# Weights and tables of five stages loaded during the stage in front of each

## The reference

```
for each layer:
    xn = layernorm(x)
    s  = attention(xn)
    g  = silu(ffn(xn))
    x  = x + s * g
```

## Time and profile before

| what | us |
|---|---|
| median of 3 runs (lowest, highest) | 6142.15 (6142.1, 6144.57) |
| the profiled execution | 6135.76 |
| its span, first to last instruction | 6134.0 |
| busy in the span: PE, DVE, ACT, POOL | 5688.0, 4321.5, 3850.9, 2914.1 |
| f0: first row load issued to last scatter begun | 1117.45 to 1221.32 |
| a1: first part load issued | 1228.42 |
| f1: first row load issued | 1976.35 |
| a2: first row load issued | 3558.97 |
| f2: first row load issued | 5439.89 |
| a3: first row load issued | 5653.05 |
| f3: first transpose | 5963.6 |

### The profile page before, as it was taken

One profiled execution on the slowest core, in us unless ns is written; L12 is line 12 of the kernel. 1 busy time (PEld: TensorE's weight loads), 2 busy tenths in 40 slices (PEclk: granted clock), 3 DMA queues, 4 the chain that ended last, 5 costly groups with the idle time before them and its releaser, 6 DMA issues. The chain is left out here.

```text
span 6134.0 us, 102245 instructions
## 1 busy us (share of the span) xinstructions
PE 5688.0 (93%) x33833; PEld 3013.5 (49%) x33833; DVE 4321.5 (70%) x9755; ACT 3850.9 (63%) x8213; POOL 2914.1 (48%) x2774
## 2 busy tenths in 40 slices
PE   8999999689997999999999979999999999987868
PEld 3444444422222566666666634444444444455558
DVE  4555555178885777777888768888888888867655
ACT  2444444256665677777777757777777777755436
POOL 1224326456776766666666533323323323324458
PEclk9999999799998999999999989999999999999879
DMA  2001001221110111111111110000000000013123
GB/s 47 15 15 39 26 15 45 75 58 40 32 35 30 42 30 34 32 32 39 40 46 46 34 35 11 13 19 11 13 19 11 13 19 11 11 43 116 45 95 97
DMA packets 304270, 219.34 MB, mean 36 GB/s; under 512 B 27890, under 2 KB 279668, under 8 KB 303492
## 3 DMA queue, kind: packets, MB, share of 16 engines
q1 hardware_dynamic: 284578, 177.38, 11.2%
q0 software_dynamic: 12544, 29.71, 1.4%
q10 hardware_dynamic: 6626, 5.72, 0.3%
HBM read 97.11 MB, written 73.87 MB: 28 GB/s over the span
## 5 line engine op out<-in xcount | busy, mean ns | idle before, releaser
L3864 PE MATMUL a_scores_ps<-a_kT,a_q_mixed 128*128 128x512 f32 x2048 | 1046.4, 593 | 3.2 <-ACT a_probs L3674 3.1
L3874 PE MATMUL a_acc_ps<-a_probsT,a_v_post 128*128 128x512 f32 x2048 | 1042.8, 592 | 0.4 <-DVE a_probsT L3767 0.4
L3674 ACT ACTIVATE a_probs<-a_scores_ps,a_neg_max 128x512 f32<-128x512 f32 x1024 | 703.0, 687 | 428.6 <-DVE a_neg_max L3757 419.3
L3757 DVE TENSOR_REDUCE a_neg_max<-a_scores_ps 128x1 f32<-128x512 f32 x1024 | 693.4, 677 | 202.0 <-PE a_scores_ps L3864 196.9
L3767 DVE STREAM_TRANSPOSE a_probsT<-a_probs 128x512 f32<-128x512 f32 x1024 | 715.5, 699 | 135.9 <-PE a_acc_ps L3874 112.5
L3679 ACT ACTIVATE a_probs<-a_probs,a_inv_sum 128x512 f32<-128x512 f32 x1024 | 727.7, 711 | 0.8 <-DVE a_inv_sum L3762 0.8
L3045 DVE TENSOR_REDUCE a_neg_max<-a_pair_ps 128x2 f32<-128x1024 f32 (+3 forms) x512 | 417.7, 824 | 354.5 <-PE a_pair_ps L3141 349.4
L2850 ACT ACTIVATE a_probsT<-a_pair_ps 128x1024 f32<-128x1024 f32 (+3 forms) x512 | 359.4, 704 | 484.4 <-PE a_pair_ps L3154 482.9
L3874 PEld LDWEIGHTS a_acc_ps<-a_probsT,a_v_post 128*128 128x128 f32 x2048 | 389.0, 190 | 490.9 <-issue 488.8
L3864 PEld LDWEIGHTS a_scores_ps<-a_kT,a_q_mixed 128*128 128x128 f32 x2048 | 384.4, 190 | 476.0 <-issue 438.2
L3620 POOL TENSOR_TENSOR a_q_mixed<-a_qT,a_pre 128x512 f32<-128x512 f32 x248 | 250.1, 1040 | 759.7 <-PE a_scores_ps L3864 759.7
(11 more groups left out here) (420 smaller groups left out, 11863.5 us busy)
## 6 DMA issues: line engine op xcount, KB each, us to landing
f_v_even<-f_v_odd SPq DMA_DIRECT2D x224, 130.0 KB, 2.3
a_v<-a_v_rows SPq DMA_DIRECT2D x256, 64.0 KB, 2.1
f_x_tiles<-routed_x SPq DMA_DIRECT2D x72, 193.0 KB
attention_out<-a_s_out SPq DMA_DIRECT2D x48, 256.0 KB, 2.3
routes_y_rows<-a_zeros SPq DMA_DIRECT2D x32, 256.0 KB, 2.8
a_parts<-routes_y_rows SPq DMA_DIRECT2D x32, 256.0 KB, 3.4
f_x<-x_after SPq DMA_DIRECT2D x32, 256.0 KB
f_gx<-x_after SPq DMA_DIRECT2D x32, 256.0 KB, 3.1
```

What stands on the lines that cost most here:

```text
L3674: act.activation(probs[:, n % NPR, :], scores_ps[n % NS][:], ACT.Exp, bias=neg_max[:, n % NS:n % NS + 1], scale=1.0, accum_out=row_sum[:, ...
L3757: dve.tensor_reduce(neg_max[:, n % NS:n % NS + 1], scores_ps[n % NS][:], AX.X, ALU.max, negate=True).then_inc(max_ready, 1)
L3864: pe.matmul(scores_ps[n % NS][:], q_mixed[:, g % 2, i].rearrange("f a q -> f (a q)"), kT[:, par, :], start=True, stop=True).then_inc(score ...
L3874: pe.matmul(acc_ps[par][:], v_post[:, g, i, :], probsT[:, g % NT, i, :], start=(p == 0), stop=(p == U - 1)).then_inc(products_done, 1)
```

## The change

A class `Ahead` holds tiles, a semaphore and a list of loads. For f0, a1, f1, a2 and a3 a function makes it before the stage in front begins, and that stage issues the loads on SP, one for each body of its loop, and waits for them at its end. The stages take their tiles from it and no longer load or wait for them, ACT issues none. w_o, w1 and w2 of f1's first layer stay in f1 (three loads behind the rows, waited for by TensorE in the second item's body), a3 keeps the load of the identity, and f2 keeps its six loads. In a3 DVE does the scaling of the query weights and the gate's norm first (without a wait), then the first rows' moments, then the rest of its set-up. The numbers of loads issued ahead are 4 in a0, 8 in f0, 11 in a1, 13 in f1 and 10 in f2.

The diff, cut to its core:

```diff
+class Ahead:
+    def __init__(self, nc, ctx, tag, shapes):
+        self.tiles = {name: ctx.enter_context(nc.sbuf_tensor(f"{tag}_{name}", shape, F32))
+                      for name, shape in shapes.items()}
+        self.loaded = nc.alloc_semaphore(f"{tag}_loaded")
+        self.loads = []
+    def take(self, names):
+        return [self.tiles[name] for name in names.split()]
+    def load(self, eng, n):
+        if 0 <= n < len(self.loads):
+            dst, src = self.loads[n]
+            eng.dma_start(dst, src).then_inc(self.loaded, 16)
+    def all_loaded(self, eng):
+        eng.wait_ge(self.loaded, 16 * len(self.loads))
+
+def dispatched_experts_weights(nc, ctx, dram):
+    ahead = Ahead(nc, ctx, "f0", {"ident": [P, P], "w1": [D, 16, P], "w2": [P, 16, D], "expert": [P, NB * NC]})
+    ident, w1, w2, expert = ahead.take("ident w1 w2 expert")
+    ahead.loads = [(ident[:], dram["ident"]), (expert[:], dram["L0f_expert"]), (w1[:], dram["L0_w1"]),
+                   (w2[:], dram["L0_w2"])]
+    return ahead
...
 a1, SP:
             load_parts(0)
-            sp.dma_start(*loads[0]).then_inc(weights, 16)
-            sp.wait_ge(parts_loaded[0], 64)
-            for dst, src in loads[2::2]:
-                sp.dma_start(dst, src).then_inc(weights, 16)
-
             load_parts(1)
             store_x(0)
             def body(j, n):
                 if n <= LAST - 3:
                     load_parts(n + 3)
+                following.load(sp, n - 1)
                 if n >= 1:
...
             bodies(sp, body)
             sp.wait_ge(x_stored, 16 * batches)
+            following.all_loaded(sp)
 a1, ACT:
-            act.wait_ge(parts_loaded[0], 64)
-            for dst, src in loads[1::2]:
-                act.dma_start(dst, src).then_inc(weights, 16)
 a1, TensorE:
-            pe.wait_ge(weights, 16 * len(loads))
 f1, SP:
             rows.load(sp, 0, 0)
-            sp.dma_start(*loads[0]).then_inc(weights, 16)
-            sp.wait_ge(rows.x_loaded, 16)
-            for dst, src in loads[2::2]:
-                sp.dma_start(dst, src).then_inc(weights, 16)
+            sp.dma_start(w_o[:, 0], dram["L1_wo"][0]).then_inc(ffn_weights, 16)
+            sp.dma_start(w1[:, 0], dram["L1_w1"][0]).then_inc(ffn_weights, 16)
+            sp.dma_start(w2[:, 0], dram["L1_w2"][:, 0]).then_inc(ffn_weights, 16)
...
                 for c in range(STEPS):
+                    if c == 1:
+                        following.load(sp, n - 4)
 f1, TensorE:
-            pe.wait_ge(weights, 16 * len(loads))
+                    if n == 1 and c == 0:
+                        pe.wait_ge(ffn_weights, 48)
 a3, SP:
             load_x(0)
-            sp.dma_start(*loads[0]).then_inc(weights, 16)
-            sp.wait_ge(x_loaded[0], 16)
-            for dst, src in loads[2::2]:
-                sp.dma_start(dst, src).then_inc(weights, 16)
+            sp.dma_start(ident[:], dram["ident"]).then_inc(ident_loaded, 16)
             for b in range(1, min(4, batches)):
                 load_x(b)
 a3, DVE:
-            dve.memset(v[:], 1.0).then_inc(pads, 1)
-            dve.wait_ge(weights, 16 * len(loads))
             dve.tensor_scalar(w_in[:, 0, :], w_in[:, 0, :], SCORE_SCALE, None, ALU.mult).then_inc(w_scaled, 1)
             chain(dve.tensor_tensor(wg_sq[:], wg[:], wg[:], ALU.mult))
             dve.tensor_reduce(wg_norm[:], wg_sq[:], AX.X, ALU.add).then_inc(gate_weights, 1)
-            dve.memset(carry[:], 0.0)
...
             moments_of(0)
+            dve.wait_ge(gate_weights, 3)
+            chain(dve.tensor_scalar(wg_norm[:], wg_norm[:], 1e-4, None, ALU.max))
+            chain(dve.reciprocal(wg_norm[:], wg_norm[:]))
+            dve.tensor_scalar(wg_unit[:], wg[:], wg_norm[:], None, ALU.mult).then_inc(gate_weights, 1)
+            dve.memset(v[:], 1.0).then_inc(pads, 1)
+            dve.memset(carry[:], 0.0)
+            dve.memset(no_counts[:], 0.0)
+            dve.tensor_copy(rows[:, :, :, HOME], home[:].rearrange("p (b c) -> p b c", c=NC)).then_inc(tails_ready, 1)
+            chain(dve.memset(fill[:], 0.0))
+            dve.memset(fill[:, HOME:HOME + 1], float(routed_rows.NOWHERE)).then_inc(fill_ready, 1)
 f2, SP:
             def body(j, n):
+                following.load(sp, n - 1)
 a0, SP:
             def body(j, n):
+                following.load(sp, n - 2)
 f0, SP:
             for g in range(4, GROUPS):
                 sp.dma_start(x[:, g], routes.x_groups[g]).then_inc(loaded[g], 16)
+            for n in range(len(following.loads)):
+                following.load(sp, n)
+            following.all_loaded(sp)
             sp.wait_ge(rows_scattered, 16 * GROUPS * NC)
 f0, ACT:
-            act.dma_start(ident[:], dram["ident"]).then_inc(weights, 16)
-            act.dma_start(expert[:], dram["L0f_expert"]).then_inc(weights, 16)
-            act.dma_start(w1[:, 0:PER * K], dram["L0_w1"][:, 0:PER * K]).then_inc(weights, 16)
-            act.dma_start(w2[:, 0:PER * K], dram["L0_w2"][:, 0:PER * K]).then_inc(weights, 16)
-            act.dma_start(w1[:, PER * K:], dram["L0_w1"][:, PER * K:]).then_inc(weights, 16)
-            act.dma_start(w2[:, PER * K:], dram["L0_w2"][:, PER * K:]).then_inc(weights, 16)
...
 program:
+    with ExitStack() as f1_ctx:
+        f1_weights = streamed_transformer_weights(nc, f1_ctx, dram)
+        with ExitStack() as a1_ctx:
+            a1_weights = paired_attention_weights(nc, a1_ctx, dram)
+            with ExitStack() as f0_ctx:
+                f0_weights = dispatched_experts_weights(nc, f0_ctx, dram)
+                causal_attention_phase(nc, dram, "a0", x_in, s, routes, batches, f0_weights)
+                dispatched_experts_phase(nc, "f0", routes, f0_weights, a1_weights)
+            paired_attention_phase(nc, "a1", x_in, x1, s, routes, batches, a1_weights, f1_weights)
+        a2_weights = mixed_attention_weights(nc, f1_ctx, dram)
+        streamed_transformer_phase(nc, dram, "f1", x1, s, x2, batches, f1_weights, a2_weights)
+        mixed_attention_phase(nc, "a2", x2, s, batches, a2_weights)
...
```

More of the change, by code:

```diff
@@ new lines, in dispatched_experts_weights, with paired_attention_weights @@
+def dispatched_experts_weights(nc, ctx, dram):
[4 more added lines that the diff above has]
+    return ahead
+def paired_attention_weights(nc, ctx, dram):
+    S, W = 8, 64
+    ahead = Ahead(nc, ctx, "a1", {"ident": [P, P], "wq": [D, S, 2, W], "wk": [D, 2, 2, 2, W], "wv": [D, D]})
+    ident, wq, wk, wv = ahead.take("ident wq wk wv")
+    ahead.loads = [(ident[:], dram["ident"]), (wv[:], dram["L1_Mv"])]
+    ahead.loads += [(wq[:, :, twice, :], dram["L1_Mq"].rearrange("d (s w) -> d s w", s=S)) for twice in range(2)]
+    k_columns = dram["L1_Mk"].rearrange("d (rho half a w) -> d rho half a w", rho=2, half=2, a=2)
+    ahead.loads += [(wk[:, :, a, half, :], k_columns[:, :, half, a, :]) for a in range(2) for half in range(2)]
+    return ahead
@@ new lines, in upper_attention_weights @@
+def upper_attention_weights(nc, ctx, dram, batches):
+    E, GR = 8, 16
+    TILES = dram["L3f_tile_no"].shape[1]
+    ahead = Ahead(nc, ctx, "a3", {
+        "w_in": [D, 3, D], "below": [P, T], "w_gate": [D, GR], "wg": [E, GR], "rank": [P, E], "place": [P, E],
+        "home": [P, batches * NC], "before": [P, P], "steps": [1, batches * NC], "tile_no": [1, TILES]})
+    w_in, below, w_gate, wg, rank = ahead.take("w_in below w_gate wg rank")
+    place, home, before, steps, tile_no = ahead.take("place home before steps tile_no")
+    ahead.loads = [(w_in[:], dram["L3_w_in"]), (below[:], dram["L3_below"]),
+                   (w_gate[:], dram["L3f_w_gate"]), (wg[:], dram["L3_ffn_wg"]), (rank[:], dram["L3f_rank"]),
+                   (place[:], dram["L3f_place"]), (home[:], dram["L3f_home"][:, 0:batches * NC]),
+                   (before[:], dram["L3f_below"]), (steps[:], dram["L3f_steps"][0:1, 0:batches * NC]),
+                   (tile_no[:], dram["L3f_tile_no"])]
+    return ahead
@@ L819, in _ @@
             pool.wait_ge(pads, 1)
-            pool.wait_ge(weights, 16 * len(loads))
             def norm(dst, b, kind, c):
@@ L898, in _ @@
         def _(act):
-            act.wait_ge(rows.x_loaded, 16)
-            for dst, src in loads[1::2]:
-                act.dma_start(dst, src).then_inc(weights, 16)
             def square(b, item, c, kind):
@@ L971, in body @@
                     if n == 0 and c == 0:
-                        act.wait_ge(weights, 16 * len(loads))
                         act.wait_ge(pads, 1)
@@ L1862, in _ @@
         def _(act):
-            act.wait_ge(x_loaded[0], 16)
-            for dst, src in loads[1::2]:
-                act.dma_start(dst, src).then_inc(weights, 16)
             act.wait_ge(pads, 1)
@@ L2137, in _ @@
         def _(pe):
-            pe.wait_ge(weights, 16 * len(loads))
+            pe.wait_ge(ident_loaded, 16)
             pe.wait_ge(pads, 1)
```

158 lines of the change are left out of this document (65 added, 93 removed).

## The result

The changed kernel took 6113.71 us (median of 5 runs, 6109.34 to 6119.54), the kernel before on the same chip 6143.69 us (5 runs, 6142.1 to 6148.51): a ratio of 0.9949 with a 95% interval of 0.9938 to 0.996, so 30 us less. The prediction was 6112.7. A later comparison of the same two kernels gave 0.9948 (0.9936 to 0.9961). The profiled execution took 6109.57 us (span 6107.7, mean granted clock 0.975; before 6135.76, 6134.0 and 0.972).

The account below looks back on a forecast made before the run. TensorE is busy for most of the span, so gains must come from waits before five stages' first useful instructions. 9.5+1.7+7.3+4.35+6.6 = 29.5 us; 6142.15-29.5 = 6112.7 us, range 6104 to 6123.

Parts of the forecast that it names:

- f0, 9.5 us forecast: First layer's experts: TensorE starts with the first row tile, not the last weights; 9.5 us gained, bounds 7.0 to 10.2.
- without a hole: First layer's experts: POOL's 64 scatters follow 1.262 us apart without interruption, so all 9.5 us reach the stage's end.
- a1, 1.7 us forecast: Second attention: without ACT's weight loads the gate runs beside DVE's product; 1.7 us gained, bounds 0.7 to 2.0.
- Rival 1: At the starts: rows land later because more loads queue behind them; 5 to 8 us lost, 6118 to 6121; chance 0.13.
- f1, 7.3 us forecast: Second layer's transformer: weights no longer awaited, DVE's table work becomes the bound; 7.3 us gained, bounds 6.3 to 7.8.
- a2, 4.35 us forecast: Third attention: TensorE starts when the rows are normalised, not at the weights; 4.35 us gained, bounds 4.0 to 4.4.
- a3, 6.6 us forecast: Fourth attention: variance ready earlier without DVE's wait for weights, moved set-up costs nothing; 6.6 us gained, bounds 5.6 to 7.0.
- The added loads, nothing forecast: Stages in front: 46 loads, 6.9 MB, on SP's queue cost nothing because SP has room; uncovered 5 to 15 us.
- rival 3: Stages in front: prefetch falls on their path, 48 us exposed against 29.5 gained, 6161 us; chance 0.02.
- rival 4: Stage starts: holes have another cause, such as code fetching, so ends do not move; about 8 us remain, 6134; chance 0.04.
- Rival 2: Inside stages: the start's gain is given back to a load, store or clock rhythm; 6124 us; chance 0.09.
- the rule: Skill page's HBM latency: rows land later under load, up to 1.8 us lost in each of a1, f1, a3; sum 24.

Follow-up runs that it names:

- the third comparison: Four unedited kernels on chip 15, against the kernel before: changed 0.9948; second attention's loads issued in first attention 0.9951; that plus parts held and first expert group alone 0.9951.
- the first pair: The first measurement and traces of the kernel before and the changed kernel, chip number not known: 6143.69 and 6113.71 us, ratio 0.9949.
- first (chip 2): Changed kernel unedited (6096.27 us, one run), and with second attention's loads back in their stage (ratio 0.9957), late in the experts before (0.9948), or in first attention (0.9947).
- second (chip 10): Kernel before (traced 6148.41 us); with only first experts' weights ahead 0.9986; changed with fourth attention's set-up first 0.9952; changed with loads moved, parts held, first group alone 0.9943.

## Why the prediction came out right, step by step

- **f0, 9.5 us forecast.** Measured 9.5 and 8.9 within a comparison, 10.4 and 10.6 between means over several, 0.2 to 0.4 over my upper bound. TensorE starts 2.8 to 3.1 us after the first load (the forecast put the first tile at 2.7 us and took 0.7 off for the tiles behind it). The first tile alone was enough. That 9.5 itself was hit is in part luck: the first trace of the kernel before has its first scatter 24.33 us after the first load, two later ones 22.95. The step "without a hole" was the weak one: read off one trace as a property of the loop, it is false in five of fourteen traces. It didn't decide, since the stalls add about as much to both kernels.
- **a1, 1.7 us forecast.** The gate runs beside VectorE's product, both from 1236.50, as forecast. The first transposes came at 14.88 us before (14.52 to 15.07, four traces) and at 13.58 in seven changed ones: 1.3. Rival 1 may have the rest: the parts land at 6.18 us (5.82 to 6.37) before and at 6.66 (6.28 to 7.18) with the second batch's loads behind them; where those are held back, 6.08 and 6.28. But the ranges overlap, and in the third comparison all four kernels have the parts at 6.27 to 6.32 us, with a gain of 1.7 (14.97 to 13.24). So a delay by the loads behind is not shown.
- **f1, 7.3 us forecast.** In the first pair the first rotation is 7.28 us earlier, and the stage's row loads are 7.32 us earlier from the fourth (84.74 us into the stage, now 77.42) to the fourteenth (7.34), while a2's loads are issued in between, one a body. That VectorE's tables, not TensorE's start, set the gain was right. Over all traces the first rotation is 6.8 us earlier in the mean (19.25 to 12.49), and the start of the last store but one as much; 5.9 us are left at the stage's end. The missing step is the drain at the end, 0.8 to 0.9 us; the other 0.5 were missing at the start.
- **a2, 4.35 us forecast.** First transposes 4.47 us earlier in the first pair, 4.2 in the mean, and 4.7 in the stage.
- **a3, 6.6 us forecast.** 6.38 us at the first transposes in the first pair, 6.6 in the mean (14.42 to 7.83). The stage shows 10.7 and 8.0; the rest goes with the clock. The order of VectorE's work is worth 0.2 to 0.3 us of it. I had given it no price of its own: with the loads ahead the set-up would have fitted into the rows' 2.9 us in either order.
- **The added loads, nothing forecast.** f2 212.4 against 212.7, f1's bodies to within 0.04 us, a0 1117.45 in both first traces: rival 3 had no place. Nor had rival 4: the ends moved with the starts.
- **"Each stage as long as before from its first transpose, within a us or two."** Wrong for a3 (290.44 to 300.51 us in three traces of the changed kernel alone) and f0 (up to 14 us). Rival 2 was right that the inside of a stage moves with the clock, in a3 and in f1's drain, and had the wrong sign for a3, where the mean gained 1.4 us more than the start. The total came out about 1 us from the forecast because such terms cancelled (f1 1.4 under its forecast, a3 1.4 over, a1 0.4 under, a2 0.4 over); that closeness is luck, the size of each start's gain is not.

The Trainium skill's page "DMA: Bandwidth & Descriptors", section "Latency and other measured facts", has an HBM access at 0.2 us on average and 2 us under high load. Here rows with more transfers close behind them landed 0.5 us later in a1's mean (0.05 in the third comparison), in a3 at 2.70 to 2.88 us (2.67 to 2.90 before), and in f1 at 2.57 to 2.92 us in eight traces and at 3.44 and 3.83 in two (2.70 to 2.91 before), so of the 5.4 us that the rule could have cost one at most came.

## What to carry to other kernels

Price a prefetch by what the stage's first useful instruction waits for next, and follow it into the loop until the distance to the old kernel is constant; at the starts that was right within 1 us in all five places. Then leave some us for what one trace can't show: before a difference inside a stage is explained, take a second trace of both kernels, in another comparison. The reordering in a3's start was worth 0.2 to 0.3 us once the loads that made it wait were gone: test such a part alone before you credit it.

## What the runs showed that was not expected

f0 has two faces. In two comparisons it ran clean in eight traces of eight, in the one between them it stalled in four of four, in the kernel before too, and in the first pair in one of two. The stalls add 11.7 to 15.6 us in four or five stretches some 20 us apart. In the one shown TensorE's products come 0.7 to 1.4 us apart, ScalarE copies a transpose 8.7 us after it ended, and the DMA engines are 5 to 11% busy, where a clean f0 has 13 to 15%. In the first changed trace no other stage has such a stretch: outside f0 TensorE is never held by "issue" for more than 0.35 us but once. It is neither a1's loads (absent in the kernel with f0's weights alone ahead) nor the early start (the kernel before stalls without it). The timed runs point the same way as the traces, and not only for single executions. The kernel before took these times:

| comparison | f0 in its traces | kernel before, median (lowest, highest), us |
|---|---|---|
| first (chip 2) | clean | 6131.12 (6125.48, 6139.11) |
| third (chip 15) | clean | 6132.87 (6119.8, 6141.65) |
| second (chip 10) | stalled | 6148.95 (6140.87, 6158.75) |
| the first pair | before clean, changed stalled | 6143.69 (6142.1, 6148.51) |

The stalled comparison is 16 to 18 us above the clean ones, about one f0's stalls (14 us). The first pair's runs lie near it, and its clean trace of the kernel before (6135.76 us) lies under all five of them. So the stall seems to hold for a chip or a session, in both kernels, and the 30 us of the result are then stalled runs against stalled runs; the one clean trace was the odd one. This is read off times, not shown by traces of those runs.

What the stall is stays open. The traces have five transfers of instructions in f0, in clean and stalled ones alike, so more fetching of code is not seen; whether the stage's code or its place in memory matters was not tried.
